# A macaron layer stack on one core: attention's matrices loaded straight to where their low parts will stand, and semaphores cleared by ranges

## The reference, cut to what matters

```
x = x + 0.5 * moe(layernorm(x), gate_w, w_gate, w_up, w_down)
x = x + attn(layernorm(x), Wq, Wk, Wv, Wg, Ws, Wo, g_norm_weight)
x = x + 0.5 * moe(layernorm(x), gate_w, w_gate, w_up, w_down)
x = x + 0.5 * ffn(layernorm(x), lut, gate_idx, up_idx, down_idx)
x = x + rec(layernorm(x), Wi, Wf, Wg, Wo, gnorm_w)
x = x + 0.5 * ffn(layernorm(x), ...)
```

## Time and profile before

| | us |
|---|---|
| three runs, median (lowest to highest) | 2729.47 (2724.72 to 2734.68) |
| the profiled execution | 2733.78 |
| its span in the trace | 2731.9 |
| router 1 (with what stands ahead of it) | 0 to 106 |
| experts 1 | 106 to 345 |
| attention | 345 to 1856 |
| router 2 | 1856 to 1955 |
| experts 2 | 1955 to 2172 |
| closing and the last block | 2172 to 2731.9 |

### The profile page before, as it was taken

The page is one execution under the profiler, slowest core; times in us unless marked ns, Lnnn a source line. Parts: engine busy times, 40 slices in busy tenths (PEclk is TensorE's granted clock), DMA queues, the critical chain, the costliest instruction groups (busy, mean ns, idle before and its releaser), DMA issues. The chain is left out here.

```text
span 2731.9 us, 44553 instructions
## 1 busy us (share of the span) xinstructions
PE 2390.3 (87%) x16926; PEld 2116.9 (77%) x16926; DVE 1798.4 (66%) x3578; ACT 865.1 (32%) x1704; POOL 1244.1 (46%) x1214
## 2 busy tenths in 40 slices
PE   6565579999999999999999999986566488999997
PEld 6444469999999999999999999976455377888886
DVE  5433358888888888888888888865422256676654
ACT  4322223333333333333333333323322132333332
POOL 3277735554555455545554555452278612222110
PEclk9988789999999999999999999995599889999999
DMA  6799710000000000000000000004599700000000
GB/s 205 236 240 228 173 26 5 17 21 20 5 17 20 21 5 17 21 20 5 16 21 17 9 17 20 13 3 134 156 242 217 153 26 24 24 24 24 16 9 16
DMA packets 196930, 169.52 MB, mean 62 GB/s; under 512 B 28944, under 2 KB 189680, under 8 KB 196208
## 3 DMA queue, kind: packets, MB, share of 16 engines
q1 hardware_dynamic: 167040, 118.69, 14.8%
q0 software_dynamic: 24576, 37.77, 7.5%
q10 hardware_dynamic: 5104, 10.22, 1.2%
HBM read 117.94 MB, written 53.13 MB: 63 GB/s over the span
## 5 line engine op out<-in xcount | busy, mean ns | idle before, releaser
L968 POOL TENSOR_TENSOR a_orstd<-a_ms,minus_half 128x8 f32<-128x8 f32 x64 | 106.8, 1669 | 492.6 <-DVE a_ms L1128 492.5
L948 POOL TENSOR_SCALAR a_pick<-a_index,lut_row 128x258 f32<-128x258 int32 x240 | 281.4, 1172 | 24.3
L1121 DVE RECIPROCAL a_rz<-a_rz 128x256 f32<-128x256 f32 x128 | 215.6, 1716 | 0.0
L776 DVE TENSOR_TENSOR e_hT<-e_psH,e_sil 128x128 f32<-128x128 f32 x128 | 37.3, 291 | 264.8 <-ACT e_sil L733 174.1
L652 PE MATMUL e_psX<-ident,e_xg 128*128 128x128 f32 x256 | 62.8, 333 | 169.1 <-DMA e_xg<-rows,slot_tok 167.6
L652 PEld LDWEIGHTS e_psX<-ident,e_xg 128*128 128x128 f32 x256 | 31.3, 159 | 217.3 <-DMA e_xg<-rows,slot_tok 212.4
L1330 PEld LDWEIGHTS a_psD<-a_v,a_at 128*128 128x128 f32 x1536 | 181.3, 192 | 7.2 <-issue 1.5
L951 POOL TENSOR_TENSOR a_found<-a_found,a_pick 128x258 f32<-128x258 f32 x240 | 177.5, 740 | 20.0
L1330 PE MATMUL a_psD<-a_v,a_at 128*128 128x128 f32 x1536 | 181.8, 275 | 1.2 <-DVE a_at L1101 1.2
L622 POOL DMA_INDIRECT e_xg<-rows,slot_tok x128 | 128.8, 1006 | 109.4 <-POOLq L247 66.1
L1101 DVE TENSOR_TENSOR a_at<-a_psB,causal 128x384 f32<-128x384 f32 x256 | 130.2, 550 | 48.8 <-PE a_psB L1267 48.8
(11 more groups left out here) (261 smaller groups left out, 7730.4 us busy)
## 6 DMA issues: line engine op xcount, KB each, us to landing
e_wg<-in_L_ffn_w_gate SPq DMA_DIRECT2D x128, 128.0 KB
e_wu<-in_L_ffn_w_up SPq DMA_DIRECT2D x128, 128.0 KB
e_wd<-in_L_ffn_w_down SPq DMA_DIRECT2D x128, 128.0 KB
rows<-r_row SPq DMA_DIRECT2D x32, 320.0 KB, 3.2
stream_b<-r_zeros SPq DMA_DIRECT2D x11, 384.0 KB, 5.7
stream_c<-rows SPq DMA_DIRECT2D x33, 128.0 KB, 3.2
r_xt<-in_L_attn_hidden_states SPq DMA_DIRECT2D x16, 256.0 KB, 3.6
stream_a<-r_xt SPq DMA_DIRECT2D x16, 256.0 KB, 4.5
```

Source lines behind the costliest of these rows:

```text
L948: nc.gpsimd.tensor_scalar(pick[:, :, :], index[:, :, :], float(c), w["lut"][:, c:c + 1], ALU.is_equal, ALU.mult).then_inc(picked, 1)
L968: nc.gpsimd.tensor_tensor(out=flat(orstd[:, :, :]), in0=ms[:, :], in1=cst["minus_half"][:, 0:TT * HQ], op=ALU.pow).then_inc(orstd_ok, 1)
L1121: nc.vector.reciprocal(rz[:, a, :], rz[:, a, :]).then_inc(rz_ok, 1)
```

## The change

There are two parts.

First, the staging tile goes. The raw matrices are loaded into tiles `w.._raw` that take the same place in SBUF as the low parts: they are allocated in a scope that is closed at once, and `w.._low` is allocated next. The high part is made from the raw tile as before, and the low part then overwrites the raw values it is made from. Since these tiles are allocated before the router, the first `EARLY_PIECES = 5` pieces (the four matrices q, k, s and v) are loaded at the end of router 1 by SyncE, behind its last copies; SyncE doesn't wait for them. The other four pieces (g and o) are loaded by ACT at experts 4, 14, 24 and 34, without a wait. Each piece has a semaphore of its own. When the conversions are made is unchanged.

Second, `Mem.clear` sorts the numbers of its semaphores and clears each unbroken range of numbers with one instruction.

```diff
@@ Mem.clear
-        for s in self.sems:
-            pool.sem_clear(s)
+        numbers = sorted(s.num for s in self.sems)
+        first = 0
+        for k in range(1, len(numbers) + 1):
+            if k == len(numbers) or numbers[k] != numbers[k - 1] + 1:
+                pool.sem_clear(range(numbers[first], numbers[k - 1] + 1))
+                first = k
@@ moe_router
                     for j in range(NJ - R, NJ):
                         keep(j)
+                    for raw, src, here in behind:
+                        sp.dma_start(raw, src).then_inc(here, 16)
                     for k in range(R):
                         sp.wait_ge(x_kept[k], 32 * (NJ // R))
@@ moe_experts
-            pieces = wide
-            stage = mem.sb("stage", [P, 2, PIECE])
-            piece_here, piece_high, piece_low = mem.sem2("piece_here"), mem.sem("piece_high"), mem.sem("piece_low")
+            pieces, load_at = wide
+            piece_high, piece_low = mem.sem("piece_high"), mem.sem("piece_low")
...
-                    act.wait_ge(piece_here[(h // 2) % 2], 16 * (h // 4 + 1))
+                    act.wait_ge(pieces[h // 2]["here"], 16)
...
-                    if e in (1, 4) and pieces:
-                        load_piece(e // 3)
+                    if pieces and e in load_at:
+                        piece = pieces[load_at[e]]
+                        act.dma_start(as_source(piece), piece["src"]).then_inc(piece["here"], 16)
...
-                    if e >= 8 and (e - 8) % 6 == 5 and (e - 8) // 6 + 2 < len(pieces):
-                        load_piece((e - 8) // 6 + 2)
@@ macaron
+            sizes = (("q", PIECE), ("k", PIECE), ("s", PIECE), ("v", WIDE), ("g", WIDE), ("o", WIDE))
+            with ExitStack() as place:
+                raw_mem = Mem(nc, place)
+                raw = {name: raw_mem.sb(f"w{name}_raw", [P, cols]) for name, cols in sizes}
+            low = {name: wmem.sb(f"w{name}_low", [P, cols], F32R) for name, cols in sizes}
...
+            early = pieces[0:EARLY_PIECES]
...
+            load_at = {4 + 10 * k: len(early) + k for k in range(len(pieces) - len(early))}
```

More of the change, by code:

```diff
@@ L36 @@
 PIECE = 2048
+EARLY_PIECES = 5
 EPS = 1e-5
@@ L136, in constants, with moe_router @@
     return c
-def moe_router(nc, cst, tag, past, x_src, gate_w, rows, fresh, slot_tok, counts):
+def moe_router(nc, cst, tag, past, x_src, gate_w, rows, fresh, slot_tok, counts, behind=()):
     HALF = NTILE // 2
@@ L538, in moe_router, with as_source @@
     return mem
+def as_source(piece):
+    return piece["raw"].rearrange("p (c n) -> p c n", n=piece["src"].shape[2])
 def moe_experts(nc, cst, tag, past, rows, w_gate, w_up, w_down, slot_tok, stream_a, stream_b, pool_dma, run, wide=None, scales_here=None, turns=None):
@@ L596, in half_of @@
         def half_of(h):
-            src, high, low, scale = pieces[h // 2]
+            piece = pieces[h // 2]
             at = slice((h % 2) * (PIECE // 2), (h % 2 + 1) * (PIECE // 2))
-            return stage[:, (h // 2) % 2, at], high[:, at], low[:, at], scale
+            return piece["raw"][:, at], piece["high"][:, at], piece["low"][:, at], piece["scale"]
         wgv = w_gate.rearrange("e (c p) f -> e p c f", p=P)
@@ L703, in high_part @@
                     nc.scalar.activation(high, raw, ACT.Copy, scale=1.0 if scale is None else scale).then_inc(piece_high, 1)
[L705 to L710, removed]
                 def rows_out(e):
@@ L1994, in macaron @@
             w = attention_weights(nc, wmem, g_norm, lut)
-            past = moe_router(nc, cst, "r1_", Mem(nc, ctx), x, gate_w, rows, (stream_a, stream_b), slot_tok, counts)
-            wide = {name: [wmem.sb(f"w{name}_{part}", [P, cols], F32R) for part in ("high", "low")]
-                    for name, cols in (("q", PIECE), ("k", PIECE), ("s", PIECE), ("v", WIDE), ("g", WIDE), ("o", WIDE))}
+            sizes = (("q", PIECE), ("k", PIECE), ("s", PIECE), ("v", WIDE), ("g", WIDE), ("o", WIDE))
[3 more added lines that the diff above has]
+            low = {name: wmem.sb(f"w{name}_low", [P, cols], F32R) for name, cols in sizes}
             pieces = []
@@ L2000, in macaron @@
                 src = src.rearrange("(h v) d -> v h d", v=DV) if name == "o" else src.rearrange("(c p) n -> p c n", p=P)
-                cut = wide[name][0].shape[1] // PIECE
+                cut = low[name].shape[1] // PIECE
                 rows_each = src.shape[1] // cut
@@ L2004, in macaron @@
                     at = slice(r * PIECE, (r + 1) * PIECE)
[L2005 to L2009, removed]
+                    pieces.append({"name": name, "at": at, "src": src[:, r * rows_each:(r + 1) * rows_each, :], "low": low[name][:, at], "raw": raw[name][:, at],
+                                   "scale": w["norm"][:, 0:1] if name == "o" else None, "here": wmem.sem(f"w{name}{r}_here")})
+            early = pieces[0:EARLY_PIECES]
+            past = moe_router(nc, cst, "r1_", Mem(nc, ctx), x, gate_w, rows, (stream_a, stream_b), slot_tok, counts,
+                              [(as_source(piece), piece["src"], piece["here"]) for piece in early])
+            high = {name: wmem.sb(f"w{name}_high", [P, cols], F32R) for name, cols in sizes}
+            for piece in pieces:
+                piece["high"] = high[piece["name"]][:, piece["at"]]
+            load_at = {4 + 10 * k: len(early) + k for k in range(len(pieces) - len(early))}
+            past = moe_experts(nc, cst, "e1_", past, rows, w_gate, w_up, w_down, slot_tok, stream_a, stream_b, pool_dma, 0, (pieces, load_at), w["here"])
+            for name, cols in sizes:
+                w[name] = [part[name][:, :].rearrange("p (c n) -> p c n", c=H if name == "o" else DC) for part in (high, low)]
             past = attention(nc, cst, w, "a_", past, stream_a, stream_b, x_att, stream_c, rows[NTOK:NTOK + P, 0:D], (gate_idx, up_idx, down_idx), looked_up)
```

## The result

The changed kernel takes 2715.27 us (median of 6 runs, 2712.73 to 2717.28), the kernel before 2731.71 (6 runs, 2724.72 to 2734.68). The ratio is 0.994 with a 95% interval of 0.9928 to 0.9952: 16.4 us less, a small gain clear of noise. The forecast was 20.1 us less; 2715.3 lies inside the range of 2698 to 2718. The profiled execution took 2715.87 us, its span is 2714.1.

The account below looks back on a forecast made before the run. GpSimd's gather and scatter, 3.19 us per expert, were taken to bound the first experts stage. Terms -13.9 (loads), 0 (start), -6.2 (clears), 0 (rest) sum to -20.1 us from a median of 2729.47: 2709 us, range 2698 to 2718.

Parts of the forecast that it names:

- Loads that leave: First experts stage, scatter 7 to 57: seven loads become three, 3.48 us each, 13.9 us less; ends 9.2 and 17.5.
- the lower end of the term: First experts stage: each of four leaving loads costs only 2.3 us, as at the stage's start, so 9.2 us less.
- the sign by which it would be off: Forecast is wrong if, among other signs, GpSimd's timeline shows losses where no load is in flight.
- Rival 3: First experts stage: losses come from ScalarE's and VectorE's conversions, not loads; only the tail counts, 2723.3 us; chance 0.08.
- The start at zero: Start of first experts stage, scatter 0 to 7: no net change from the early loads, 2.5 us either way.
- SyncE's path: Router 1's end: five load issues by SyncE, through at 104.9 if the queue holds 0.7 MB, cost nothing.
- The sign named for the cover: Router 1's end: SyncE's wait for PE's side of the barrier, 10.8 us before, shrinks but stays above zero.
- The clears: Last block: four clear instructions in place of 91, at 71 ns each, save 6.2 us; other clears count zero.
- Rival 2: Semaphore clears cost by the semaphore, not the instruction, so a range of 66 takes as long; 2715.6 us, chance 0.06.
- The seventh gather: Both experts stages: 66 clears hold this gather back 2.4 us; its gain set at zero, lower end -4.8 us.
- rival 4: Experts' start: expert 0's weights land only after all 5.24 MB and PE stands; 2742 us at 100 GB/s, chance 0.04.
- The rule of turns between queues: Experts' start: with pieces on SyncE's queue POOL has one competitor, not two, gaining nearly all of 4.7 us; not adopted.

Follow-up runs that it names:

- the two kernels with both kinds of loss removed: Changed kernel with low part made from PSUM and no attention load in experts 1: all nine pieces at router's end, 2709.87 us; four inside router's loop, 2712.64 us.
- clears only: Kernel before with the range clears alone, loads and placement as before: 2726.38 us, ratio 0.999.
- old schedule: Changed kernel with no early piece, all nine loads issued by ScalarE at the experts used before: 2723.69 us, ratio 0.9971 to the kernel before.
- after twice: Changed kernel, profiled once and then once more unchanged: 2715.27 us, then 2715.75 us.
- loads only: Changed kernel with one clear for each semaphore as before, so new placement and loads alone: 2720.68 us, ratio 0.9971 to the kernel before.
- nine early: Changed kernel with all nine pieces loaded at the first router's end in place of five: 2715.91 us, ratio 0.9945 to the kernel before.
- late loads on SyncE: Changed kernel with the four late loads issued by SyncE behind the weights of experts 12, 22, 32 and 42, not by ScalarE: 2719.82 us, one run.
- the last version: Changed kernel with each late piece cut into eight 128 KB transfers and the low part made from PSUM: 2703.93 us, ratio 0.9905 to the kernel before.

## Why the prediction was right, and where it was off

**The bound** was read rightly. GpSimd's pace of 3.19 us is what the stage falls back to, and in the two kernels with both kinds of loss removed the stretch comes to 159.8 and 160.5.

**Loads that leave: the mechanism was right, the term too large.** The forecast had 13.9 us. Over three profiles each (before, clears only, old schedule; after twice, loads only), the stretch is 182.8 with the old schedule and 173.7 with the new one: 9.1 us. Two steps made it too large. The 3.48 us for a load came from dividing the whole loss of 24.4 by seven loads, but 9.4 of it was lengthening by low parts, and the change leaves their number as it was. The idle time alone is 14.6 on average with seven loads and 7.8 with three: 6.8 less, 1.7 for each load that leaves. And the sum was made on one profile that lay above the mean of its kind (182.8). The other 2.1 of the 9.1 are lengthening, 9.0 on average with the old schedule and 6.8 with the new. No run shows that the change has a part in it; the averages of three profiles can differ by so much by chance. So it is partly luck that the lower end of the term, 9.2, is what came: it priced a load at 2.3 us, and 4 x 2.3 holds no lengthening. The prediction named the sign by which it would be off, losses where no load is in flight, and the scatter at 302.22 is one. Rival 3, that the losses were the conversions', had a small chance for all of the loss; it was true of more than a third of it (9.4 of 24.4).

**The start at zero** held: scatter 0 at 117.47 for 118.25, and 26.4 for 27.0 to scatter 7. The loads ran faster than the 340 to 387 GB/s assumed, at up to 430, and ended near 106 to 108 as estimated.

**SyncE's path** was safer than computed: the five issues were through at 93.7, not 104.9. The estimate held that 0.7 MB fit into the queue. With nine early, seven pieces (7.3 MB) were issued in 4.2 us, in which the engines move 1.8 MB at 430 GB/s, so the queue took some 5.5 MB: what holds SyncE is not bytes in flight. The sign named for the cover was off as well. SyncE's wait for PE stayed at 10.8 us instead of shrinking; the issues took their time out of its wait for its own last copies, 3.9 us before and 0.2 after.

**The clears**: 6.2 forecast, 5.7 measured, since a range clear takes 88 to 347 ns and not 71. Rival 2, a price by the semaphore, falls: one clear of a range of 66 took 398 ns. That the measured time, 2715.3, is the one that this rival named (2715.6) is chance. The stages behind the other clears start no earlier for having fewer, as set. The seventh gather's 2.5 us bought nothing, as set too. In the kernel before the clears did hold that gather, but 66 clears need not (see the loads alone); this has no effect on the sum.

**The sum** with the measured sizes: 9.1 for the stretch, 0.3 for all ahead of it (the scatter of 7 comes at 144.6 with the old schedule and at 144.3 with the new, over the same three profiles each) and 5.7 behind: 15.1 us, against 16.4 measured, whose interval goes from 13.1 to 19.7. The forecast of 2709 started from a median of 2729.47 in three runs. Over six runs the kernel before has 2731.71, so 2.2 of the 6.3 us between 2709 and 2715.3 lie in the starting point.

**Slower** (rival 4) didn't come with five pieces. Its mechanism, weights that land late behind the pieces, was seen with nine, where it cost the start some 10 us, though the kernel as a whole was still faster than before.

**The rule of turns between queues.** The prediction weighed the Trainium skill's rule (the page "DMA: Bandwidth & Descriptors", its section "Queues, rings and completion order") that each DMA engine goes round the queues with work, by which a load on SyncE's queue would hurt GpSimd less than one on ScalarE's. The run with the late loads on SyncE shows idle time of 9.3 us where 6.6 to 9.7 were: no gain.

**Left open**: why lengthening differs between 6.4 and 11.1 us for the same conversions (how they happen to meet GpSimd's transfers would do it, but no run steers that), the 4.9 us of idle time in the last version, and what holds up single clears in one kernel and not in another.

## What to carry to other kernels

Where one engine's back-to-back instructions set the pace, split its loss into idle time ahead of instructions and instructions that run longer, before dividing it by a suspected cause; the two had different causes here. Moving a large load into a stretch where the DMA engines are idle is worth the idle time that it made, as long as what is queued behind it isn't needed soon. Cutting a load into small ones over many steps can be worth as much as moving it.

## What the runs showed of the hardware

A VectorE subtraction of two SBUF tiles (128 x 1024, float32) lengthens a GpSimd indirect transfer that begins while it runs, by nearly the time that the two overlap: the one at 280.04 began 1.15 us before the subtraction's end and took 1.02 longer. A transfer that began first was not lengthened, nor was the subtraction: 16 of the 18 in the kernel after began while a transfer ran, and took 1.21 to 1.28 us. With one input in PSUM there was no such effect in the 18 halves of each of four kernels. The Trainium skill ("SBUF — State Buffer", section "SBUF: two separate sides") says that VectorE and GpSimd share a pair of SBUF ports which one instruction holds alone, and counts a VectorE operation with two SBUF inputs among those that take it, though only against a GpSimd operation that reads SBUF. The transfers here read their table `slot_tok` from SBUF; no run shows whether this read is what waits. That the GpSimd side is held up, the trace agrees; that the loser always waits is not seen for VectorE, whose 1.22 us stayed the same.

Seven loads of 1 MB in rows of 4 or 8 KB were issued within 4.2 us; two of Wo, in rows of 1 KB, then held SyncE for 14.33 us. The eight stores of the router, also in rows of 1 KB, were held too (6.81 us). This suggests that the queue's limit is a number of rows, which no run here varied alone.

The early loads alone, with nothing of the router's left in the queues, ran at 416 to 430 GB/s (96 to 104 after). The router's own loads and stores had gone at 340 to 387 at the same DMA share of about 1.
